# A decoder layer on one core: end 1 a stage ahead, the last cross-attention takes more in, the last batch routed between the first expert slots

## The reference

```
x = layernorm(x + self_attention(x))             # 16 heads of 16
x = layernorm(x + cross_attention(x, ctx))       # ctx: 4 x 64 tokens, 16 heads of 16, with biases
p = softmax(x @ router_w.T); top 2 of 8 experts  # per token
x = layernorm(x + sum over the two: p_e * gelu(x @ w1[e].T) @ w2[e].T)   # hidden 1024
```

## Time and profile before

| | |
|---|---|
| median of 3 runs | 833.93 us (832.22 to 837.69) |
| the profiled execution | 835.05 us, its span 833.3 us |
| mean granted TensorE clock | 0.934 of full |
| busy: PE, DVE, ACT, POOL | 721.4, 334.6, 287.4, 220.5 us |
| DMA | 92.84 MB, mean 111 GB/s |

### The profile page before, as it was taken

How to read it: one execution, slowest core, us unless ns; L and a number is a source line. 1 busy time by engine, 2 the same in 40 slices (tenths; PEclk the granted TensorE clock), 3 DMA queues, 4 the chain that set the end, 5 groups by cost and what they waited for, 6 DMA issues and landing times.

```text
span 833.3 us, 11591 instructions
## 1 busy us (share of the span) xinstructions
PE 721.4 (87%) x3964; PEld 468.3 (56%) x3965; DVE 334.6 (40%) x762; ACT 287.4 (34%) x525; POOL 220.5 (26%) x280
## 2 busy tenths in 40 slices
PE   6899999999998679897978646599999999999970
PEld 3322333322224253646545435599999999999960
DVE  3687876788964460726535343000000000000004
ACT  2246656666774315252433212011111111111112
POOL 2211111110135301010140444233333333333322
PEclk9869999999999899999999667699999999999995
DMA  5974033434341300001030758366776665566506
GB/s 160 178 181 83 7 84 70 78 84 98 51 141 51 128 25 1 1 1 50 1 52 0 170 139 226 58 186 185 189 187 180 163 164 168 174 185 178 169 11 201
DMA packets 58910, 92.84 MB, mean 111 GB/s; under 512 B 13841, under 2 KB 45298, under 8 KB 57331
## 3 DMA queue, kind: packets, MB, share of 16 engines
q1 hardware_dynamic: 50355, 83.86, 37.2%
q0 software_dynamic: 8512, 8.44, 6.4%
HBM read 75.94 MB, written 17.86 MB: 113 GB/s over the span
## 4 chain that ended last, share of the span: by engine, by line
PE 73%; DVE 9%; ACT 5%; DMA 5%; issue 4%; POOL 2%; SPq 1%; POOLq 0%; DVEq 0%; ACTq 0%
PE ps L1773 16%; PE ps L1762 16%; PE ps L1481 7%; PE ps L1472 7%; PE ps L1406 6%; PE ps L1510 3%; DVE nmx L1019 2%; PE ps L1424 2%; PE ps L1593 2%; ACT probs L848 2%; POOL metas L752 2%; PE ps L1631 1%; PE ps L1493 1%; PE ps L1621 1%; PE ps L1624 1%
## 5 line engine op out<-in xcount | busy, mean ns | idle before, releaser
L848 ACT ACTIVATE probs<-ps 128x512 f32<-128x512 f32 x256 | 136.0, 603 | 102.3 <-PE ps L1472 101.7
L1019 DVE TENSOR_REDUCE nmx<-ps 128x1 f32<-128x512 f32 x256 | 159.7, 681 | 15.3 <-PE ps L1406 14.6
L1762 PEld LDWEIGHTS ps<-xtT,w1c 128*128 128x128 f32 x1248 | 146.8, 193 | 4.2 <-issue 2.2
L1762 PE MATMUL ps<-xtT,w1c 128*128 128x128 f32 x1248 | 147.2, 277 | 1.7 <-ACT xtT L972 1.7
L1773 PE MATMUL ps<-wexp,hidT 128*128 x624 | 143.8, 384 | 0.3 <-issue 0.3
L1369 DVE TENSOR_SCALAR yw<-ps,mt 128x256 f32<-128x256 f32 x39 | 18.9, 484 | 268.7 <-PE ps L1773 268.7
L1773 PEld LDWEIGHTS ps<-wexp,hidT 128*128 128x128 f32 x624 | 117.5, 193 | 15.6 <-issue 0.7
L978 ACT ACTIVATE hidT<-ps 128x1024 f32<-128x1024 f32 x39 | 39.9, 1024 | 233.4 <-PE ps L1762 229.4
L793 POOL DMA_INDIRECT acc<-yw,mt x39 | 61.9, 1587 | 177.0 <-DVE yw L1369 175.0
L1406 PE MATMUL ps<-kst,qst 96*128 96x512 bf16 x256 | 98.8, 409 | 4.8 <-DVE nmx L1019 2.9
L1472 PE MATMUL ps<-qst,kst 99*128 99x512 bf16 x256 | 93.7, 389 | 1.0 <-ACT probs L848 0.7
(11 more groups left out here) (204 smaller groups left out, 781.6 us busy)
## 6 DMA issues: line engine op xcount, KB each, us to landing
w1c<-in_w1T SPq DMA_DIRECT2D x39, 1024.0 KB
wexp<-in_w2T SPq DMA_DIRECT2D x8, 1024.0 KB
kst<-scrk SPq DMA_DIRECT2D x48, 128.0 KB, 7.1
qst<-scrq SPq DMA_DIRECT2D x8, 384.0 KB, 4.8
xTb<-in_xT SPq DMA_DIRECT2D x4, 512.0 KB, 7.7
qst<-scrq SPq DMA_DIRECT2D x8, 256.0 KB, 5.5
xr<-in_x SPq DMA_DIRECT2D x4, 512.0 KB, 5.1
x2d<-xr SPq DMA_DIRECT2D x4, 512.0 KB, 3.5
```

Source lines behind the costliest of these rows:

```text
L848: act.activation(probs[n % 8][:, :], ps[:, 4 + n % 3, :], ACT.Exp).then_inc(s_exp, 1)
L1019: dve.tensor_reduce(nmx[w % 2][:, k:k + 1], ps[:, ring_bank("max", w, k), :], AX.X, ALU.max, negate=True).then_inc(s_mfree, 1)
L1762: mm = pe.matmul(ps[:, 2 * (j % 2) + f // 4, f % 4 * P:(f % 4 + 1) * P], w1c[j % 2][:, k * FF + f * P:k * FF + (f + 1) * P], xtT[j % 2][:, ...
```

## The change

- **Stages on PE, ACT, DVE and POOL.** End 1 of batch n+1 stands in stage n (before: of batch n), while x, e2 and r are still n-1, n-2 and n-3. `turn_x(0, n)` and `q2_proj(n)` stay in stage n but move to an earlier place, among the max tiles. There are four stages (n from 0 to 3).
- **`last_cross`** holds cross-attention of batch 3, end 2 of batch 2, and routing of batches 1 and 2 (before: end 2 of batch 2 and routing of batch 1; batch 2 was routed in a stage with end 2 of batch 3).
- **`last_end`** holds end 2 of batch 3, with the last steps of the routing of batch 2 and `plan_early` on DVE.
- **Batch 3** is turned, routed and counted between the first slots: `turn_tile(0)`, `turn_x(1, 3)`, `hidden(0)`, `turn_tile(1)`, `logits(3)`, `hidden(1)`, `expert_out(0)`, `turn_tile(2)`, `positions(3)`, slot 1, `count`. On POOL its `scatter_metas` no longer stands between gather 1 and gather 2, but half after scatter 1 and half after scatter 2. On DVE `plan_rest` comes after the weighing of slot 1.
- **Memory.** `qh` and `ql` have one buffer each; `ybuf2` and `xTs2` take the place of weights used only earlier; `max2_turn` writes another bank. So `load_expert` takes experts 0, 1, 6, 7, 4 after self-attention, and 2, 3, 5 after the last cross-attention; `store_x2(2)` comes behind these three (before: behind expert 2 alone).

The core of the diff:

```diff
-            e1, x, e2, r = (n - k if 0 <= n - k < NB else None for k in range(4))
+            e1, x, e2, r = (n - k if 0 <= n - k < NB else None for k in (-1, 1, 2, 3))
...
@@ SP
-        for e in (0, 1, 7):
+        for e in (0, 1, 6, 7):
             load_expert(e)
+        sp.wait_ge(s_k2h, KD)
+        sp.wait_ge(s_k2l, KD)
+        load_expert(4)
         store_x2(0)
         store_x2(1)
         sp.wait_ge(s_pv2, NU * NB)
-        load_expert(2)
+        for e in (2, 3, 5):
+            load_expert(e)
         store_x2(2)
-        for e in range(3, 7):
-            load_expert(e)
@@ POOL
-        for t in range(2):
+        for t in range(3):
             gather(t)
-        scatter_metas(NB - 1)
-        gather(2)
...
             scatter(t)
+            if 1 <= t <= 2:
+                scatter_metas(NB - 1, (t - 1,))
@@ PE, q2_proj and exp2_tile
-            pe.wait_ge(s_exp2, max(NP * b - 1 + m, 0))
+            if b > 0:
+                pe.wait_ge(s_m2f, NP * (b - 1) + 7 + m)
+            if b > 1:
+                pe.wait_ge(s_exp2, NP * (b - 1))
...
             pe.wait_ge(s_m2c, b + 1)
+            if b + 1 < NB:
+                pe.wait_ge(s_q2t, KD * (b + 2))
@@ PE, after the stages
+        for n in range(NB):
+            stage(n)
+        last_cross()
+        end_step(1, 3, 0)
+        positions(2)
+        end_step(1, 3, 1)
+        count(2, 6, 0)
+        for step in range(2, QT + 2):
+            end_step(1, 3, step)
...
         turn_tile(0, 0, 0)
+        turn_x(1, 3, 0)
+        turn_x(1, 3, 1)
+        pe.wait_ge(s_rt, RT * (NB - 1))
         hidden(0, 0, 0)
-        positions(NB - 1)
         turn_tile(1, 1, 0)
+        logits(3, range(QT))
         hidden(1, 1, 0)
-        count(NB - 1, 7, 128)
-        turn_tile(2, 0, 1)
         pe.wait_ge(s_we, 16 * NE)
         expert_out(0, 0)
-        for j in range(1, 4):
+        turn_tile(2, 0, 1)
+        positions(3)
+        tile(1, 1, 0)
+        count(3, 7, 128)
+        for j in range(2, 4):
             tile(j, j, 0)
@@ DVE, after last_cross
+            norm_o(1, 3, 0)
+            slots(2)
+            norm_o(1, 3, 1)
+            plan_early()
+            norm_o(1, 3, 2)
+            add_residual(1, 3, 0)
+            norm_o(1, 3, 3)
+            for t in range(1, QT):
+                add_residual(1, 3, t)
```

More of the change, by code:

```diff
@@ L212, in decoder_layer @@
     bq4_s = sb("bq4_s", KD, F32, LATE)
+    kept = place[LATE]
+    xwk_s = sb("xwk_s", wn, F32, LATE)
+    xwv_s = sb("xwv_s", wn, F32, LATE)
+    ctx_s = sb("ctx_s", wn, F32, LATE)
+    bv_s = sb("bv_s", D, F32, LATE)
+    assert place[LATE] <= R_K + 48 * KB
+    place[LATE] = kept
+    ybuf2 = [sb(f"ybuf2_{i}", D, F32, LATE) for i in range(QT)]
+    xTs2 = sb("xTs2", KD * S, F32, LATE)
     assert place[LATE] <= R_K + 48 * KB
@@ L961, in stage, with last_cross @@
                 normalise(1, e2)
-        for n in range(NB + 3):
+        for n in range(NB):
             stage(n)
-        act.activation(ahead[:, 2:3], ahead[:, 1:2], ACT.Gelu)
+        def last_cross():
+            copy_xT(1, 1, 0)
+            copy_xT(1, 1, 1)
+            copy_o2(1, 2, 0)
+            copy_o2(1, 2, 1)
+            copy_o2(1, 2, 2)
+            router_exp(1)
+            copy_o2(1, 2, 3)
+            exp2(3, 0)
+            exp2(3, 1)
+            normalise(1, 2)
+            exp2(3, 2)
+            exp2(3, 3)
+            copy_xT(1, 2, 0)
+            copy_xT(1, 2, 1)
+            o2_out(3, 0)
+            exp2(3, 4)
+            exp2(3, 5)
+            o2_out(3, 1)
+            exp2(3, 6)
+            exp2(3, 7)
+            o2_out(3, 2)
+            router_exp(2)
+            o2_out(3, 3)
+        last_cross()
+        for t in range(QT):
+            copy_o2(1, 3, t)
+        normalise(1, 3)
         def copy_xtT(t, j):
@@ L1302, in stage @@
         def stage(n):
-            e1, x, e2, r = (n - k if 0 <= n - k < NB else None for k in range(4))
-            if e1 is not None and n > 0:
+            e1, x, e2, r = (n - k if 0 <= n - k < NB else None for k in (-1, 1, 2, 3))
+            if e1 is not None:
                 norm_o(0, e1, 0)
@@ L1351, in stage, with last_cross, last_end @@
                 add_residual(1, e2, 1)
-            if r == NB - 2:
-                plan_early()
-            if e2 is not None:
                 add_residual(1, e2, 2)
                 add_residual(1, e2, 3)
-            if e1 is not None:
-                q2_low(e1)
-        for n in range(NB + 3):
+            q2_low(n)
+        for n in range(NB):
             stage(n)
-        plan_rest()
+        def last_cross():
+            norm_o(1, 2, 0)
+            row_max2(3, 0)
+            row_max2(3, 1)
+            norm_o(1, 2, 1)
+            row_max2(3, 2)
+            row_max2(3, 3)
+            router_logits(1)
+            norm_o(1, 2, 2)
+            add_residual(1, 2, 0)
+            row_max2(3, 4)
+            row_max2(3, 5)
+            probabilities(1)
+            norm_o(1, 2, 3)
+            add_residual(1, 2, 1)
+            row_max2(3, 6)
+            row_max2(3, 7)
+            max2_parts(3)
+            choose(1, 0)
+            add_residual(1, 2, 2)
+            add_residual(1, 2, 3)
+            max2_T(3)
+            second_choice(1)
+            slots(1)
+            router_logits(2)
+            probabilities(2)
+            choose(2, 0)
+            second_choice(2)
+        def last_end():
+            norm_o(1, 3, 0)
[7 more added lines that the diff above has]
+                add_residual(1, 3, t)
+        last_cross()
+        last_end()
+        router_logits(3)
+        probabilities(3)
+        choose(3, 0)
+        second_choice(3)
+        slots(3)
         def weigh(t):
@@ L1374, in _ @@
                 weigh(t)
+                if t == 1:
+                    plan_rest()
         for b in range(NB):
```

180 lines of the change are left out of this document (103 added, 77 removed).

## The result

The changed kernel took 822.28 us (median of four runs, 821.51 to 825.95); the kernel before took 835.81 beside it (832.22 to 840.38). The ratio is 0.984 with a 95% interval of 0.980 to 0.988: 13.5 us faster, where I had forecast 27 and a range of 795 to 821. One execution in all that follows, of x8_all_batch2_out (820.3 us), was in a slower state of the chip and is left out. The profiled execution took 821.51 us, its span 819.7, at a mean clock of 0.931.

The account below looks back on a forecast made before the run. PE was taken to bound the expert slots, with idle time to win before them. Terms -2.7, -9.3, -5.9, -14.2 and +5 sum to -27.1 us: 835.05 profiled to 807.9, 806.8 from the median, given as 807; range 795 to 821.

Parts of the forecast that it names:

- Stages and last cross: Stages 0 to 3 and batch 3's cross-attention: 176.7 instead of 179.4 us, -2.7, bounds -9 to +6.
- Gap to end 2: Between the last cross and end 2 of batch 3: 0.8 us left of 10.1, -9.3.
- End 2 to the first tile: End 2 of batch 3 to the first turned tile: 26.2 instead of 32.1 us, -5.9, bounds -8.5 to -3.5.
- First tile to second hidden: First turned tile to second hidden product: 18.1 instead of 32.3 us, -14.2, bounds -17 to -8.
- In the slots: Expert slots: table writes make gathers 5 and 6 late, waits of 2.4 to 5 us; +5, bounds 0 to +10.
- the fifth rival: Expert slots: waits keep PE's clock at half, making the kernel slower than before, say 843 us; chance 0.03.
- The first: Before gather 0: slow DMA of loads and stores makes the hand-over 10 us late, 817 us; chance 0.13.
- The second rival: Stage ends: the single qh's 4.5 us chain stays uncovered at three of them, about 9 us more, 816; chance 0.08.
- The fourth: Slots start early but PE waits there for gathers, weights or routing, giving back 14.2 us, 821; chance 0.03.

Follow-up runs that it names:

- x8_all_batch2_out: x7 with batch 2's turns, logits and router's exponential also put back behind the last weighting, as in x3; 813.7 us, ratio 0.971.
- x13: The changed kernel plus 15 matmuls into an unread bank, ten before end 2 of batch 2's last output projection, five before the first exponential tile; 814.2 us, ratio 0.974.
- x3: The changed kernel with batch 2's turns, copies, logits and exponential put back behind the last weighting; 820.3 us, ratio 0.978.
- x10: The changed kernel with the last cross and last end 2 in the earlier kernel's stage order; 822.6 us, ratio 0.980.
- x12: The changed kernel with only its last part undone: batch 3 routed before the first slots, its eight table writes ahead of gather 2; 830.8 us, ratio 0.990.
- x2: The changed kernel with batch 3's table writes two at a time behind scatters 1 to 4, not four behind 1 and 2; 818.9 us, ratio 0.975.
- x1: The changed kernel with tile 2's residual sum ahead of the split of the maxima and choose(1, 0) behind the copy to mT2; 813.3 us, ratio 0.968.
- x4: The changed kernel with DVE waiting for end 2's normalisation factors before it takes ql in stages 2 and 3; 822.7 us, ratio 0.980.
- x5: The changed kernel measured again, unaltered, on a second chip; 820.4 us, ratio 0.982.
- x7: x1, x2 and x4 together on the changed kernel, with probabilities(1) also behind max2_T(3); 812.5 us, ratio 0.970.
- x6: x1 with only batch 2's logits moved behind the last weighting; 820.6 us, ratio 0.981.
- x9: x7 with only batch 2's logits moved behind the last weighting, as in x6; 809.7 us, ratio 0.964.
- x14: x9 plus filler matmuls, 11 each at the starts of stage 3 and the last cross, 4 and 5 ahead of the exponentials; 805.0 us, ratio 0.961.
- x15: x14 plus 34 filler matmuls in the wait for the first gather; 803.7 us, ratio 0.962.
- x11: The changed kernel with the earlier order in the last cross only, batch 2's turn and logits between the last end 2's first steps, plus x2's and x4's edits; 824.0 us, ratio 0.982.

## Why the prediction was too fast

The direction held (faster, 0.94), the size was half of it: -13.6 for -27.1 us. By the steps of the sum:

- **Stages and last cross: forecast -2.7, measured +7.7. This is the step that failed**, and in it one sentence: "The half clock stays after the longest waits only; I take 2.5 us." PE's idle time was right, 25.8 us (148.7 busy and 28.0 idle were forecast); busy time was 161.3. With 146.2 of plain work, the half clock cost 15.1 us instead of 2.5. For the last cross the walk gave 28.50 plus 3.2 of work and 4.7 idle, 36.4 us; it took 45.95, and the other four stretches 141.1 where 140.3 were left. So nearly all of this step's miss, and 9.6 of the 13.5 us in all, is one stretch. x13 shows the cause of most of it: with the waits filled, 6.5 us come back. The rows of before at hand were the eight query matmuls at 5.82 instead of 3.70 behind short waits in stage 0: I priced that loss where it stood, and took no such loss for a stretch whose clock had been 1.00. But the change takes the interleaved end 2 out from between the exponentials and puts a chain of DVE steps ahead of them.
- **Gap to end 2: -9.3, measured -9.3**, and worth next to nothing in all: x3 and x10 have the gap back, in part and whole, and take the same time as the changed kernel. The term was right and its price stood in another term.
- **End 2 to the first tile: -5.9, measured -5.5** (26.66 for 26.2). The slots were written 2.3 us behind the first transpose, not 3.6; the table chain took 24.4 us from there, not 22.6.
- **First tile to second hidden: -14.2, measured -14.8**, and 17.4 by x12's difference. `hidden(0)` began at half clock, as forecast, but took 4.62, not 5.3.
- **In the slots: +5, measured +8.3.** The mechanism was as described: table writes ahead of gather 5, a wait of 3.63 us, then an expert output at half clock. I had priced the wait at 2.4 to 5 and named the half-clock output (2.8 us) as a "perhaps" that the 5 left no room for. By x2 (300.1 beside 303.0 and 305.3) 3 to 5 us of it belong to the table writes in fours; x12, which undoes the whole part, has 297.0, and what the last 3 us are isn't shown. The clock recovers within one slot, as I had argued against the fifth rival.
- **Rivals.** The first didn't happen: gather 0 waited for the table. The DMA moved 267, 354 and 199 GB/s in the three stretches of 5 us from 470, together the 4.1 MB of loads and stores, and 22 in the next; the gather went at 492.50. So the stores were there either way, and no run shows whether they could have passed the loads. The second rival didn't happen either; PE's wait at stages 3 and 4 was 3.86 us instead of 2.8, for another reason (last section). The fourth gave the number, 821, but by another mechanism. What I lacked was a rival in which the clock falls in the last cross. Two of the prices were summed wrong: 4.5 us open three times instead of 1.5 once is 12 us and not 9 (819, not 816), and 1% slower than before takes 4.9 slots at half clock, not 5.2; neither moves the range. And the 2.3 us of waiting that I cited for a fall has a row at full length behind it (0.66 at 377.08); the next turn, at 378.64, took 1.08.

End 1 a stage ahead was never undone alone. Its worth is worked out only: x10 differs from before by it and by the slots' part, 15.2 us in the medians, and the slots' part is 8.5 to 10.4; 5 to 7 are left. Batch 3's first maximum tile, 429.1 us before and 424.3 in x10, says 4.8.

## What to carry to other kernels

Where a stretch runs at full clock and small pieces of another chain stand in its waits, taking these out can cost more than the work that they are: price a rewritten order once at each clock level, and treat a stretch at 1.00 as something that can be lost. When the granted clock looks like the cause, fill the waits with matmuls into an unused bank before reordering anything; it is one small edit, and it tells clock from waiting. Here it was also a repair as good as the best reordering (814.2 and 813.3), and the two together gave the fastest kernels. And when small DMAs are moved into a pipelined loop, put in as many per turn as the issuing engine has room for, since the gathers queue behind them.

## What the runs showed of the hardware

**A fall without a wait.** Batch 2's 16 logits matmuls (8 columns each, 1.95 us, PE marked busy throughout) were followed by the lower level, 1.8 to 3.2 us after they began, in each of the eight executions that had them among the exponentials (changed, x1, x2, x4, x5, x7, x12, x13), with no wait between; in x3, x6, x8, x9, x14 and x15, where they stand behind, the clock held until the last weighting had ended. The busy share of PE doesn't show this. But the same 16 matmuls don't do it everywhere. In the last cross of the changed kernel batch 1's logits stand among the row-maximum tiles, and the clock holds behind them, up to the first fall:

```profile
428.54 1.84 PE L1735 MATMUL ps<-rw_s,xTs 128*128 128x8 f32 x16
...
432.03 0.39 PE L1695 MATMUL ps<-k2l,qh 128*128 128x512 f32 x1
```

Batches 0 and 1 have their logits among such tiles in each of the 17 traces, 34 times in all; within 5 us the clock fell behind them twice (batch 0 in x14 and x15). What else the place among the exponentials adds isn't shown.

**A slow return.** In the changed kernel PE worked without a pause from 444.11 to 457.42 before the exponentials' matmuls went from 0.63 to 0.39 us. In x10 the low stretch lasted some 7 us, in x9 some 11. Why x10 fell, and x11 and the kernel before didn't, all with the interleaved order and waits of 1.42 and 0.84 us ahead of the exponentials, I can't say from these rows; what of PE's past decides stays open.

**GpSimd beside VectorE.** In the changed kernel the reciprocal root runs beside the remainder `ql`:

```profile
416.44 1.22 DVE L1190 TENSOR_TENSOR ql<-q2t,qh 128x1024 fp32r<-128x1024 f32 x1
...
416.62 1.92 POOL L747 TENSOR_TENSOR rstd<-ve,halves 128x4 f32<-128x4 f32 x1 [27.80 <-DVE nm L1171]
...
419.99 1.11 PE L1672 MATMUL ps<-identf,xr 128*128 128x128 f32 x4 [3.86 <-ACT xr L893]
```

With x4's edit, which lets `ql` start later:

```profile
416.24 1.02 POOL L747 TENSOR_TENSOR rstd<-ve,halves 128x4 f32<-128x4 f32 x1 [27.80 <-DVE nm L1171]
...
417.57 1.23 DVE L1190 TENSOR_TENSOR ql<-q2t,qh 128x1024 fp32r<-128x1024 f32 x1 [1.41 <-POOL nmr L749]
```

A step on four columns takes 1.92 us instead of 1.02, and with normalisation behind it PE waits 0.9 us longer. `ql` ends at 417.66; 1.02 behind that is 418.68, and `rstd` ended at 418.54, about as if it had done nothing until then; the other two such pairs in this trace give 0.16 and 0.17 us. The Trainium skill (SBUF — State Buffer, SBUF: two separate sides) says that a VectorE operation with two SBUF inputs and a GpSimd operation that reads SBUF take a shared port pair as an exclusive lock, and that whichever starts first has it for the whole instruction; these three pairs agree, within 0.17 us.
